# Expert order, per-expert release of weight buffers, and the gate's top-2 in one piece

## The reference

```python
x = x + attn(layernorm(x), W_qkv, W_proj, b_proj)
x = x + ffn(layernorm(x), gate_w, gate_b, expert_w, expert_b)

# attn: q = exp(-q*q/2), k = exp(-k*k/2), kv = k^T v per head
#       out = (q kv) / (q . sum(k) + 1e-6), then out @ W_proj.T + b_proj
# ffn:
logits = einsum('bsd,ed->bse', x, gate_w) + gate_b
topv, topi = top_k(logits, 2)          # the others are set to -inf
gate_score = softmax(logits)
expert_out = einsum('bsd,edo->bseo', x, expert_w) + expert_b
out = einsum('bseo,bse->bso', expert_out, gate_score)
```

## Time and profile before

| what | value |
|---|---|
| time, median of 2 runs | 3658.64 us (3657.54 to 3659.74) |
| time of the profiled execution | 3689.15 us |
| span of its cores 0 to 7 | 3687.6, 3681.8, 3669.3, 3667.1, 3647.7, 3655.9, 3655.0, 3642.1 us |
| PE matmul busy | 3158.9 us, 86% of the span |
| DVE, ACT, POOL busy | 1092.1, 670.1, 135.4 us |
| DMA | 229.63 MB, 62 GB/s on average |
| expert matmuls | 2 x 4096, 1825.8 us busy |

### The profile page before, as it was taken

One profiled execution on the slowest core, in us unless ns is written; L12 is line 12 of the kernel. 1 busy time (PEld: TensorE's weight loads), 2 busy tenths in 40 slices (PEclk: granted clock), 3 DMA queues, 4 the chain that ended last, 5 costly groups with the idle time before them and its releaser, 6 DMA issues.

```text
span 3687.6 us, 45034 instructions; the slowest of 8 cores (3642.1 to 3687.6 us)
## 1 busy us (share of the span) xinstructions
PE 3158.9 (86%) x18304; PEld 1513.0 (41%) x18304; DVE 1092.1 (30%) x1580; ACT 670.1 (18%) x1121; POOL 135.4 (4%) x166
## 2 busy tenths in 40 slices
PE   4988499999498869999869886999993988599998
PEld 2444244444244434444324443444441444344443
DVE  2334322222233442222141344222212334422221
ACT  2544100000254410000034441000002444200000
POOL 0000000000000000000000000000000000000000
PEclk8989699999698869999979886899996998699999
DMA  9061861111601061111240006111116010611111
GB/s 183 1 160 54 147 204 18 18 18 24 183 1 47 24 206 18 18 18 23 61 140 16 31 24 206 18 18 18 18 18 188 1 46 10 219 18 18 18 19 22
DMA packets 74203, 229.63 MB, mean 62 GB/s; under 512 B 9298, under 2 KB 25682, under 8 KB 68754
## 3 DMA queue, kind: packets, MB, share of 16 engines
q0 software_dynamic: 37664, 58.94, 11.6%
q1 hardware_dynamic: 33890, 130.06, 10.7%
q10 hardware_dynamic: 2448, 37.75, 3.2%
HBM read 159.76 MB, written 92.27 MB: 68 GB/s over the span
## 4 chain that ended last, share of the span: by engine, by line
PE 76%; DVE 6%; DMA 5%; SPq 4%; issue 4%; ACT 4%; DVEq 0%; ACTq 0%; another core or an unknown queue 0%; POOL 0%; POOLq 0%
PE pb L127 74%; SPq L127 4%; PE pbt L127 2%; DMA sel<-sel 2%; ACT ktmp L127 2%; DVE st L127 2%; DMA wkv_s<-wkvT 1%; DVE attB L127 1%; DMA wkv_s<-scr_wkv 1%; ACT attA L127 1%; DMA out<-xres 1%; DVE lnx L127 1%; DVE r_all L127 0%; ACT q_s L127 0%; ACT lnx L127 0%
## 5 line engine op out<-in xcount | busy, mean ns | idle before, releaser
L127 PE MATMUL pb<-we,lhsT_lo 128*128 128x512 bf16 x4096 | 917.6, 386 | 4.3 <-DVE lhsT_lo L127 4.3
L127 PE MATMUL pb<-we,lhsT_hi 128*128 128x512 bf16 x4096 | 908.2, 383 | 0.0
L127 PEld LDWEIGHTS pb<-we,lhsT_lo 128*128 128x128 bf16 x4096 | 401.0, 99 | 518.4 <-issue 89.0
L127 PEld LDWEIGHTS pb<-we,lhsT_hi 128*128 128x128 bf16 x4096 | 403.9, 99 | 493.9 <-issue 45.2
L127 PE MATMUL pb<-wkv_s,lnx 128*128 128x512 bf16 x2048 | 471.6, 393 | 66.5 <-DMA wkv_s<-scr_wkv 42.2
L127 ACT ACTIVATE q_s<-xres 128x1024 bf16<-128x1024 f32 x128 | 135.2, 1057 | 1866.4 <-DMA xres<-x 1547.1
L127 DVE TENSOR_TENSOR lhsT_hi<-lnx,z 128x4096 bf16<-128x4096 bf16 x64 | 146.7, 2292 | 704.9 <-PE pb L127 704.9
L127 PEld LDWEIGHTS pb<-wkv_s,lnx 128*128 128x128 bf16 x2048 | 203.8, 101 | 327.4 <-issue 106.1
L127 DVE TENSOR_TENSOR lhsT_lo<-lnx,z 128x4096 bf16<-128x4096 bf16 x64 | 146.7, 2292 | 638.1 <-PE pb L127 637.7
L127 PE MATMUL pb<-wp_s,attA 128*128 128x512 bf16 x1024 | 258.0, 397 | 0.0
L127 PE MATMUL pb<-lnx,wq_s 128*128 128x512 bf16 x1024 | 228.0, 382 | 11.7 <-ACT ktmp L127 9.9
(11 more groups left out here) (72 smaller groups left out, 1566.0 us busy)
## 6 DMA issues: line engine op xcount, KB each, us to landing
we<-scr_we SPq DMA_DIRECT2D x24, 2048.0 KB, 14.2
xres<-x SPq DMA_DIRECT2D x16, 2048.0 KB, 27.5
out<-xres SPq DMA_DIRECT2D x64, 512.0 KB, 15.5
out<-otmp POOLq DMA_DIRECT2D x128, 256.0 KB, 5.1
we<-ew POOLq DMA_DIRECT2D x8, 2048.0 KB, 35.8
scr_we<-we ACTq DMA_DIRECT2D x8, 2048.0 KB, 28.5
wkv_s<-scr_wkv SPq DMA_DIRECT2D x12, 1024.0 KB, 22.8
wq_s<-scr_wq ACTq DMA_DIRECT2D x3, 2048.0 KB, 14.6
```

The source lines that it names most:

```text
L127: last = getattr(eng, name)(*a, **kw)
```

## The change

Three things are changed together.

- In f_em the experts run in the order 6, 7, 0, 1, 2, 3, 4, 5 (those that lie on xres first). PE signals after each expert, and each expert's buffer is noted as read by its own signal. A half (lhsT_lo, lhsT_hi) is noted as read when the last of its four experts has run.
- The top-2 runs once for all 16 tiles, after the last gate copy, with the same operations on 128x128 (and 128x16) operands; the four groups of score transposes follow it, each waiting for all of "gate".
- The regions gate_c0 to gate_c3 and sbf_c0 to sbf_c3 fall away; "gate" takes their place.

```diff
@@ f_em @@
-                for e in range(E):
+                eorder = (list(range(self.n_in_c2, E))
+                          + list(range(self.n_in_c2)))
+                half_left = {0: sum(1 for e in eorder if e < EH),
+                             1: sum(1 for e in eorder if e >= EH)}
+                for idx, e in enumerate(eorder):
                     half = e // EH
...
-                                stop=(e == E - 1 and dt == DT - 1))
-                    if e == EH - 1 or e == E - 1:
-                        i = k.inc(last_inst, "s_pe")
+                                stop=(idx == E - 1 and dt == DT - 1))
+                    i = k.inc(last_inst, "s_pe")
+                    k.note_r(f"we{e}", "s_pe", i)
+                    half_left[half] -= 1
+                    if half_left[half] == 0:
                         k.note_r(lhname, "s_pe", i)
-                        if e == E - 1:
-                            for bank in banks:
-                                k.note_w(f"bank{bank}", "s_pe", i)
-                            for ee in range(E):
-                                k.note_r(f"we{ee}", "s_pe", i)
-                            k.note_r("scoresT", "s_pe", i)
-                            k.note_r("eb_s", "s_pe", i)
+                    if idx == E - 1:
+                        for bank in banks:
+                            k.note_w(f"bank{bank}", "s_pe", i)
+                        k.note_r("scoresT", "s_pe", i)
+                        k.note_r("eb_s", "s_pe", i)
@@ the gate loop @@
-            if t % TPC == TPC - 1:
-                emit_top2(ch)
-                for t4 in range(0, NT, 4):
-                    if t4 not in st_done and \
-                            min(NCH, (t4 + 4 + TPC - 1) // TPC) - 1 <= ch - 1:
-                        st_done.add(t4)
-                        emit_st(t4)
@@ behind the loop, the expert loads of stage D and flush_we_notes @@
+        def f_t2(eng):
+            k.wait_w(eng, "vector", "gate")
+            k.inc(eng.tensor_reduce(
+                k.m1.ap(), v3(k.lgraw.ap()), axis=AX.X, op=ALU.max), "s_v")
...
+        self.on("vector", f_t2)
...
+        self.on("vector", f_sbf)
         for t4 in range(0, NT, 4):
-            if t4 not in st_done:
-                emit_st(t4)
+            def f_st(eng, t4=t4):
+                k.wait_w(eng, "tensor", "gate")
...
+            self.on("tensor", f_st)
...
+            self.on("vector", f_ste)
```

More of the change, by code:

```diff
@@ L1203, in emit_batch @@
         self.merge_region("ktmp1", "gate")
[L1205 to L1320, removed]
@@ L1348, in emit_batch, with f_ge @@
             self.on("tensor", f_g)
-            def f_ge(eng, t=t, ch=ch, bank=bank):
+            def f_ge(eng, t=t, bank=bank):
                 k.wait_w(eng, "vector", f"bank{bank}")
@@ L1378, in emit_batch, with v3 @@
         self.flush_we_notes()
-        for t4 in range(0, NT, 4):
-            if t4 not in st_done:
-                emit_st(t4)
+        def v3(ap):
+            return ap.rearrange("p (t e) -> p t e", e=E)
+        def f_t2(eng):
+            k.wait_w(eng, "vector", "gate")
+            k.inc(eng.tensor_reduce(
+                k.m1.ap(), v3(k.lgraw.ap()), axis=AX.X, op=ALU.max), "s_v")
+            k.wait(eng, "vector", "s_v", k.cnt("s_v"))
+            k.inc(eng.tensor_tensor(
+                v3(k.gt1.ap()), v3(k.lgraw.ap()),
+                k.m1.ap().unsqueeze(2).broadcast_to([128, NT, E]),
+                op=ALU.is_equal), "s_v")
+            k.wait(eng, "vector", "s_v", k.cnt("s_v"))
+            k.inc(eng.scalar_tensor_tensor(
+                k.gt2.ap(), k.gt1.ap(), -1e30, k.lgraw.ap(),
+                op0=ALU.mult, op1=ALU.add), "s_v")
+            k.wait(eng, "vector", "s_v", k.cnt("s_v"))
+            k.inc(eng.tensor_reduce(
+                k.m2.ap(), v3(k.gt2.ap()), axis=AX.X, op=ALU.max), "s_v")
+            k.wait(eng, "vector", "s_v", k.cnt("s_v"))
+            i = k.inc(eng.tensor_tensor(
+                k.ed.ap(), k.m2.ap(), k.m1.ap(), op=ALU.subtract), "s_v")
+            k.note_w("gate", "s_v", i)
@@ new lines, in emit_batch, with f_t2s, f_t2b @@
+        self.on("vector", f_t2)
+        def f_t2s(eng):
+            k.wait_w(eng, "scalar", "gate")
+            i = k.inc(eng.activation(k.ed.ap(), k.ed.ap(), AF.Exp), "s_sc")
+            k.note_w("gate", "s_sc", i)
+        self.on("scalar", f_t2s)
+        def f_t2b(eng):
+            k.wait_w(eng, "vector", "gate")
+            k.inc(eng.tensor_scalar(
+                k.rden.ap(), k.ed.ap(), scalar1=1.0, scalar2=None,
+                op0=ALU.add), "s_v")
+            k.wait(eng, "vector", "s_v", k.cnt("s_v"))
+            k.inc(eng.reciprocal(k.rden.ap(), k.rden.ap()), "s_v")
+            k.inc(eng.tensor_tensor(
+                v3(k.gt1.ap()), v3(k.lgraw.ap()),
+                k.m2.ap().unsqueeze(2).broadcast_to([128, NT, E]),
+                op=ALU.is_ge), "s_v")
+            i = k.inc(eng.tensor_tensor(
+                v3(k.gt2.ap()), v3(k.lgraw.ap()),
+                k.m1.ap().unsqueeze(2).broadcast_to([128, NT, E]),
+                op=ALU.subtract), "s_v")
+            k.note_w("gate", "s_v", i)
@@ new lines, in emit_batch, with f_t2e, f_t2f @@
+        self.on("vector", f_t2b)
+        def f_t2e(eng):
+            k.wait_w(eng, "scalar", "gate")
+            i = k.inc(eng.activation(k.gt2.ap(), k.gt2.ap(), AF.Exp), "s_sc")
+            k.note_w("gate", "s_sc", i)
+        self.on("scalar", f_t2e)
+        def f_t2f(eng):
+            k.wait_w(eng, "vector", "gate")
+            k.inc(eng.tensor_tensor(
+                k.gt2.ap(), k.gt2.ap(), k.gt1.ap(), op=ALU.mult), "s_v")
+            k.wait(eng, "vector", "s_v", k.cnt("s_v"))
+            i = k.inc(eng.tensor_tensor(
+                v3(k.scores.ap()), v3(k.gt2.ap()),
+                k.rden.ap().unsqueeze(2).broadcast_to([128, NT, E]),
+                op=ALU.mult), "s_v")
+            k.note_w("gate", "s_v", i)
+            k.note_w("scores_done", "s_v", i)
@@ new lines, in emit_batch, with f_sbf, f_ste @@
+        self.on("vector", f_t2f)
+        def f_sbf(eng):
+            k.wait_w(eng, "vector", "gate")
+            i = k.inc(eng.tensor_copy(
+                k.scores_bf.ap(), k.scores.ap()), "s_v")
+            k.note_w("gate", "s_v", i)
+        self.on("vector", f_sbf)
+        for t4 in range(0, NT, 4):
+            def f_st(eng, t4=t4):
+                k.wait_w(eng, "tensor", "gate")
+                k.wait_w(eng, "tensor", "ident")
+                k.wait_rw(eng, "tensor", "bank6")
+                for j in range(min(4, NT - t4)):
+                    t = t4 + j
+                    inst = eng.transpose(
+                        k.pbt[0].ap()[0:E, j * 128:(j + 1) * 128],
+                        k.scores_bf.ap()[:, t * E:(t + 1) * E],
+                        k.ident.ap())
+                i = k.inc(inst, "s_pe")
+                k.note_w("bank6", "s_pe", i)
+                k.note_r("gate", "s_pe", i)
+            self.on("tensor", f_st)
+            def f_ste(eng, t4=t4):
+                nj = min(4, NT - t4)
+                k.wait_w(eng, "vector", "bank6")
+                k.wait_rw(eng, "vector", "scoresT")
+                i = k.inc(eng.tensor_copy(
+                    k.scoresT.ap()[0:E, t4 * 128:t4 * 128 + nj * 128],
+                    k.pbt[0].ap()[0:E, 0:nj * 128]), "s_v")
+                k.note_r("bank6", "s_v", i)
+                k.note_w("scoresT", "s_v", i)
+                k.note_w(f"scoresT_g{t4 // 4}", "s_v", i)
+            self.on("vector", f_ste)
@@ L1538, in emit_batch @@
         self.merge_region("gate", "ktmp1")
-        for ch in range(NCH):
-            self.merge_region(f"gate_c{ch}", "ktmp0")
-            self.merge_region(f"gate_c{ch}", "ktmp1")
-            self.merge_region(f"sbf_c{ch}", "ktmp0")
-            self.merge_region(f"sbf_c{ch}", "ktmp1")
         ewsz = DT * O * 2
@@ L1637 @@
 _NC_CACHE = {}
+from concourse.bass_utils import run_bass_kernel_spmd
+_NC_CACHE = {}
 def _get_program():
```

2 lines of the change are left out of this document (removed).

## The result

| what | before | after |
|---|---|---|
| time, median | 3659.13 us (10 runs) | 3744.91 us (11 runs) |
| ratio, after to before | | 1.0246, 95% interval 1.0205 to 1.0287 |
| span of the profiled execution, slowest core | 3687.6 us | 3743.3 us |
| PE busy | 3158.9 us | 3160.1 us |

The change makes the kernel 86 us slower by the medians and 90 us by the ratio (75 to 105). The forecast was 3714 us in a range of 3676 to 3752. Some executions of any kernel here run with one die at a lower clock; ratios and comparisons leave them out.

A forecast was written before the change was run, and what follows sets the result against it. PE, busy 86%, was taken to bound the expert stages and DMA bytes the sequence boundaries. Stalls +104, first tiles +2 and +21, boundaries -72, gate 0 gave +55 us on the median 3658.6: 3714 us, range 3676 to 3752.

The forecast's parts named there:

- Wrong if the clock in expert windows falls below 1.00: Sign against the forecast: granted PE clock under 1.00 in trace windows of the expert stages after the change.
- 60 stalls at lhsT_hi: At 60 tile changes PE waits 1.74 us while DVE rewrites the single lhsT_hi buffer: +104 us, bounds 96 to 114.
- first tiles: Each sequence's first tile waits: 2.2 us for lhsT_hi in the first, about 7 us for experts 6, 7 in the others.
- three boundaries: Between sequences, buffers freed per expert let the next loads start earlier: 24 us three times, -72 us, range -57 to -90.
- gate: Top-2 in one piece ends before sel8's DMA lands, so it is worth nothing; bounds 0 and +5 us.
- The clock falls at each tile change: Rival: PE restarts at 1.2 GHz after every stall, 2.2 us 60 times, +132 us, 3846 in all; chance 0.06.
- x 3 waits for the last otmp write, which is as late as before and now behind less: Boundary step: the fourth x chunk's load still waits for that write; the estimate took 280 GB/s and 24 us gained.
- The boundary gains nothing: Rival: an overlooked wait in SP's queue holds the next sequence's loads until the end; +127, 3786 us; chance 0.09.
- The stall isn't there: Rival: lhsT_hi is rewritten under cover, so only the boundary counts; -49, 3610 us; chance 0.05.
- with 30 us and no wait in the first tiles: Further case of the no-stall rival: 30 us gained per boundary, 3582 us (-2.1%); a third of its 0.05 beyond 2%.

The follow-up runs named there:

- Experiment 3: Changed kernel with a second buffer for lhsT_hi, used by odd tiles; ratio 0.9881 to the kernel before, times 3622 to 3630 us.
- experiment 6: Kernel before with readers noted per expert and the new expert order in each sequence's last tile alone; ratio 0.9895, 3604 to 3613 us but for one.
- Experiment 8: Experiment 6 with the last wkv_s quarter loaded ahead of x chunk 3 on SP's queue; ratio 0.9835, times 3582 to 3601 us.
- experiment 9: Experiment 6 with all four wkv_s quarters right behind x chunk 0 on SP's queue; ratio 0.9887, times 3585, 3590 and 3631 us.
- experiment 4: Changed kernel with 26 unused PE transposes between bias matmuls and the wait for lhsT_hi; ratio 1.0145 to the kernel before, 3717 to 3723 us.
- experiment 5: Changed kernel with the old expert order in each sequence's first tile alone; ratio 1.0190 to the kernel before, times 3716 and 3724 us.
- experiment 7: Kernel before with readers noted per expert, old expert order and old gate; ratio 0.9877, times 3605 and 3607 us.
- experiment 11: Experiment 9 with the second buffer for lhsT_hi; ratio 0.9802 to the kernel before, times 3577 to 3582 us.

## Why the prediction was right or wrong

The range held the time and the side was right, with 31 us missing in the sum, of which the table finds 27. That the range held is in part luck. A term that the prediction had put outside its range, the clock, cost 23 us, and there was room for it only because the stalls came out near their lower bound and the range had been drawn for all bounds at once; the interval of the ratio (3734 to 3764 us) reaches past its end of 3752. One of the prediction's own signs of being wrong came up: "Wrong if the clock in expert windows falls below 1.00". Step by step:

| step | predicted | shown |
|---|---|---|
| 60 stalls at lhsT_hi | +104 | +97: pitch 30.33 for 28.71 us, 1.62 each |
| clock behind the stalls | 0 (rival: +132) | +23: 15 of 60 tiles, 1.56 us each |
| first tiles | +23 | +20: DVE 2.2, DMA 21.3 less the 1.07 us waited there before, three times |
| three boundaries | -72 | -58: gaps 197.5 to 139.3 us |
| gate | 0 | 0: 1.0018 (0.9993 to 1.0043) |
| sum | +55 | +82, measured +86 |

**Stalls: right.** DVE's start at the last lhsT_hi matmul, 2.29 us of work and 0.14 us to PE's start (0.26 was assumed) give 1.62 us. Experiment 3 shows the buffer to be the cause.

**The clock: the failed step.** The prediction put "The clock falls at each tile change" against one row, 2.31 us of standing still at a granted clock of 1.00, and took it as all or nothing, 0.06 for 132 us. One row can't decide it, since equal stalls go either way: of the 60 stalls 15 were followed by a stretch at half clock, and of 96 lone stalls of 2.01 us (experiments 6, 8, 9) 69 were and 27 weren't. The right term was 1.56 us for every fourth tile. The sentence of the Trainium skill that was weighed there ("TensorE: Matmul & The Clock Gate", section "A second HAM failure mode: psum-queue depth-cycling") had the kind of effect right; the trace agrees with it as to the swinging, and gives the size, 23 us and not 132. Experiments 3 and 4 show that the stall and not memory or the die is the cause.

**First tiles: right**, in mechanism and size (8.3, 8.1 and 5.0 us for 7 each); experiment 5 takes them away.

**The boundary: right in mechanism, 14 of 72 us too large.** "x 3 waits for the last otmp write, which is as late as before and now behind less" was the weak sentence. otmp landed 19 us after it was issued, chunk 3 and the last quarter of wkv_s stood behind it, and DMA ran at 0.67 to 0.71 of its time in the last 20 us, where the estimate had 280 GB/s to the end. Experiment 8, which takes the last quarter out of that place, shortens the gap; its gain in time is not clear of noise. The mean of all cores has the gaps fall from 190 to 134 us, so the 58 isn't an accident of two cores. The rival "The boundary gains nothing" is refuted. What the prediction didn't see is that the two releases have different worth: most of the gain, by the means of all cores some 47 of 56 us, comes from noting the readers one by one and needs no new order (experiment 7).

**The rival "The stall isn't there"** fell with the first row of waits, and experiment 3 shows what it would have been worth: 3615 us by ratio, with the 3610 of the prediction beside it. (The 3582 us beside that, "with 30 us and no wait in the first tiles", doesn't come out of its terms: 3658.6 - 90 is 3569, and with the lower bounds of the first tiles 3580. Nothing rests on it but the third of a chance of 0.05.)

**Open:** why the sum of the three gaps differs by 6 to 20 us among the cores of one execution (the 7 us more at the first boundary of core 3 is of that kind, cores 0 and 1 have 43 us there); why the release alone gives so much; how much of experiment 11 is due to each of its parts; and why the clock falls behind some stalls and not behind others.

## What to carry to other kernels

Before an order is turned round so that a buffer is free sooner, look at which buffer is then both last in one round and first in the next: a single buffer rewritten under cover of the other half loses its cover, here 1.6 us sixty times and the clock after it. Note readers as finely as they are known first; that cost nothing and gave most of the gain, and an order that serves the end of a stage is needed in its last round alone, if it pays for its stall there. A rival that one row speaks against keeps its chance until more than one row of the kind has been read. Where a better order of transfers brings nothing, look at each engine's queue for an item that waits for the late transfer ahead of work that doesn't need it, before the bytes are blamed.

## What the runs showed of the hardware that was not expected

Behind 15 of 60 idle times of 1.57 to 2.0 us the granted TensorE clock fell to half for part of the next tile (0.89, 0.50, 0.75 in successive windows of 2 us) and cost 1.56 us each; behind the others the tiles kept their 30.33 us. On all 8 cores the falls lay four tiles apart, now and then five. A lone idle time of 2.01 us, behind more than 400 us of work without a stop, was followed by such a stretch in 69 of 96 cases. 26 transposes of no use in the idle time removed every one of these long tiles, on every core. So the length of the idle time alone doesn't tell whether the clock falls.
